# Startup loads of a linear-attention and FFN kernel: pieces over all 128 partitions, another order on the queues

## The reference

```
q = exp(x Wq.T + bq);  k = exp(x Wk.T + bk);  v = x Wv.T + bv
kv = cumsum over tokens of (k outer v);  k1 = cumsum over tokens of k
attention = (q . kv) / (q . k1), per head;  x = layernorm(x + attention Wo.T + bo)
h = ((x w) a1) a2;  x = layernorm(x + tanh(h + bias))
```

## Time and profile before

| | |
|---|---|
| median of three runs | 2304.31 us |
| the profiled execution | 2303.22 us |
| its span, first to last instruction | 2301.4 us |
| PE busy | 2241.9 us (97%) |
| DVE busy | 1617.2 us (70%) |
| POOL busy | 1294.2 us (56%) |
| ACT busy | 1012.3 us (44%) |
| mean granted clock of TensorE | 0.993 |
| DMA: share of 16 engines | 33.3% on SP's queue, 0.3% on ACT's |

### The profile page before, as it was taken

One profiled execution on the slowest core, in us unless ns is written; L12 is line 12 of the kernel. 1 busy time (PEld: TensorE's weight loads), 2 busy tenths in 40 slices (PEclk: granted clock), 3 DMA queues, 4 the chain that ended last, 5 costly groups with the idle time before them and its releaser, 6 DMA issues.

```text
span 2301.4 us, 77308 instructions
## 1 busy us (share of the span) xinstructions
PE 2241.9 (97%) x27752; PEld 1829.6 (80%) x27752; DVE 1617.2 (70%) x2456; ACT 1012.3 (44%) x1695; POOL 1294.2 (56%) x1797
## 2 busy tenths in 40 slices
PE   7999999999999999999999999999999999999985
PEld 6778888888888888888888888888888888887864
DVE  5576776776776776776776776776776776767674
ACT  4344444444444444444444444444444444444432
POOL 1356556556556556556556555555555555555554
PEclk9999999999999999999999999999999999999997
DMA  7133333333333333333333333333333333333221
GB/s 183 57 110 111 104 111 111 103 111 112 103 110 112 103 111 111 102 111 112 102 109 114 103 110 112 103 111 111 104 112 109 105 108 112 106 103 108 71 70 56
DMA packets 294574, 243.17 MB, mean 106 GB/s; under 512 B 33424, under 2 KB 225936, under 8 KB 294288
## 3 DMA queue, kind: packets, MB, share of 16 engines
q1 hardware_dynamic: 293136, 236.59, 33.3%
q10 hardware_dynamic: 1152, 2.10, 0.3%
HBM read 139.99 MB, written 98.57 MB: 104 GB/s over the span
## 4 chain that ended last, share of the span: by engine, by line
PE 95%; DVE 2%; issue 1%; SPq 1%; ACT 1%; DMA 1%; POOL 0%; POOLq 0%; DVEq 0%; ACTq 0%
PE SC L326 26%; PE SC L328 25%; PE SC L327 25%; PE SC L417 6%; PE ND L393 5%; PE ND L384 3%; PE ND L380 2%; PE ND L428 2%; DVE o L803 1%; DMA WK<-wT 0%; SPq L253 0%; ACT A L648 0%; DVE WK L816 0%; SPq L241 0%; PE ND L327 0%
## 5 line engine op out<-in xcount | busy, mean ns | idle before, releaser
L916 POOL TENSOR_SCALAR_AFFINE_SELECT A<-A 128x512 f32<-128x512 f32 x512 | 331.8, 682 | 321.1 <-ACT A L648 321.0
L803 DVE RECIPROCAL o<-ND 128x512 f32<-128x512 f32 x128 | 427.8, 3342 | 0.1
L857 DVE TENSOR_TENSOR xres<-SC,xres 128x512 f32<-128x512 f32 x128 | 88.5, 692 | 431.8 <-PE SC L328 431.6
L910 POOL TENSOR_TENSOR oL<-o,oH 128x512 fp32r<-128x512 f32 x128 | 166.4, 1300 | 327.0 <-ACT oH L627 327.0
L638 ACT ACTIVATE WK<-xres,shift,rstd 128x512 f32<-128x512 f32 x128 | 104.1, 814 | 531.7 <-POOL shift L951 531.7
L648 ACT ACTIVATE A<-SC 128x512 f32<-128x512 f32 x512 | 264.7, 603 | 43.3 <-PE SC L417 43.3
L326 PE MATMUL SC<-xTH,WqH 128*128 128x512 f32 x512 | 210.8, 412 | 9.5 <-ACT QT L598 3.7
L326 PE MATMUL SC<-WfH,x1H 128*128 128x512 f32 x512 | 201.0, 393 | 14.4 <-issue 7.9
L816 DVE TENSOR_TENSOR_SCAN WK<-ones,k,KT 128x128 f32<-128x128 f32 x512 | 207.5, 467 | 7.1 <-PE ND L380 6.8
L326 PE MATMUL SC<-WoH,oH 128*128 128x512 f32 x512 | 201.1, 393 | 11.3 <-issue 9.3
L598 ACT ACTIVATE QT<-SC,bcol 128x512 f32<-128x512 f32 x128 | 88.4, 690 | 270.4 <-PE SC L328 270.4
(11 more groups left out here) (103 smaller groups left out, 4983.3 us busy)
## 6 DMA issues: line engine op xcount, KB each, us to landing
xres<-x SPq DMA_DIRECT2D x128, 256.0 KB, 2.6
x_rows<-WK SPq DMA_DIRECT2D x128, 256.0 KB, 3.1
WK<-x_rows SPq DMA_DIRECT2D x512, 64.0 KB, 2.0
out<-WK SPq DMA_DIRECT2D x128, 256.0 KB, 2.0
xin<-x SPq DMA_DIRECT2D x504, 64.0 KB, 1.9
k_rows<-WK SPq DMA_DIRECT2D x120, 256.0 KB, 2.0
WK<-k_rows SPq DMA_DIRECT2D x480, 64.0 KB, 2.2
A<-a1T ACTq DMA_DIRECT2D x4, 256.0 KB, 5.4
```

Of the source, the lines that this page charges most:

```text
L803: nc.vector.reciprocal(o[:, :, :], den_ps).then_inc(recip_ready, 1)
L857: nc.vector.tensor_tensor(r, oproj_ps, r, ALU.add).then_inc(r_ready, 1)
L910: nc.gpsimd.tensor_tensor(oL[:, :, :], o[:, :, :], oH[:, :, :].bitcast(F32), ALU.subtract).then_inc(ol_ready, 1)
L916: last = nc.gpsimd.affine_select(out=A[:, k % 2, j, :, :], in_=A[:, k % 2, j, :, :], compare_op=ALU.is_ge, fill=0.0, base=0, pattern=[[0, ...
```

## The change

Every piece of x and of the four attention weights now fills all 128 partitions. A piece of x is one block of 32 tokens with its 4 feature groups: the source walks over 4 groups outermost, 32 tokens inside, 512 bytes each, and lands in 128 partitions by 512 bytes. A piece of a weight is one of four row sets: 4 groups outermost, 32 rows inside, 2048 bytes each, and lands in 128 partitions by 2048 bytes. Number and size of the pieces are the same. This holds for x in the loop as well.

SP now issues quarter 0 of a1T and a2, x 0, quarter 1, x 1, quarter 2, x 2, quarter 3, x 3, and then the biases, w, x 4, x 5, Wv, Wo and the rest as before. ACT issues Wq between its splits of quarters 0 and 1, and Wk behind that of quarter 1. ACT's `split_w` comes behind its first `keep_k`. DVE's `split_w` comes behind its `split_a12` and `turn_x` of tile 4, and its `split_wq_wk` 2 ahead of `turn_x` of tile 5.

```diff
@@ -45,7 +45,7 @@
     assert B == 2 * QUAD and NI >= 4
 
     x_t = x.rearrange("b (i p) d -> b i p d", p=P)
-    x_b = x.rearrange("b (i t p) (a f) -> b i a p t f", t=P // HD, p=HD, a=HG)
+    x_b = x.rearrange("b (i t p) (a f) -> b i t a p f", t=P // HD, p=HD, a=HG)
 
     k_rows = nc.dram_tensor("k_rows", [P, D], F32).ap()
     x1_rows = nc.dram_tensor("x1_rows", [P, D], F32).ap()
@@ -161,6 +161,12 @@
             early = c.static() and B * c.it + m in (2, 3)
             return V[:, m % 2, :] if early else xin[:, m % XIN, :]
 
+        def load_blocks(engine, tile, a, semaphore):
+
+            rows = a.rearrange("(a f p) n -> f a p n", a=HG, p=HD)
+            for f in range(NK):
+                engine.dma_start(tile[:, f, :], rows[f]).then_inc(semaphore, 16)
+
         def blocks_by_group(a):
             return a.rearrange("p (a m q) -> p m a q", a=HG, q=HD)
 
@@ -235,11 +241,6 @@
 
         @block.sync
         def _(sp):
-            def load_by_block(tile, a, semaphore):
-                rows = a.rearrange("(a f p) n -> a p f n", a=HG, p=HD)
-                for j in range(HG):
-                    sp.dma_start(tile[j * HD:(j + 1) * HD], rows[j]).then_inc(semaphore, 16)
-
             def load_biases():
                 sp.dma_start(bcol[:, 0, :], bq).then_inc(biases_loaded, 16)
                 sp.dma_start(bcol[:, 1, :], bk).then_inc(biases_loaded, 16)
@@ -249,9 +250,9 @@
                                      ).then_inc(biases_loaded, 16)
 
             def load_x(c, n):
-                for j in range(HG):
-                    sp.dma_start(x_buffer(c, n)[j * HD:(j + 1) * HD, :].rearrange("p (t f) -> p t f", t=HG),
-                                 x_b[n % B, c.it + n // B, j]).then_inc(xin_loaded[n % B], 16)
+                for t in range(HG):
+                    sp.dma_start(x_buffer(c, n)[:, t * P:(t + 1) * P],
+                                 x_b[n % B, c.it + n // B, t]).then_inc(xin_loaded[n % B], 16)
 
             def slot(c, k):
                 if c.exists(k - 2):
@@ -290,22 +291,28 @@
                     wait_before(sp, (out_ready, c.count(n + 1)))
                     sp.dma_start(out_t[n % B, c.it + n // B], y[:, n % 2, :]).then_inc(out_stored[n % B], 16)
 
+            def load_aux(f):
+                sp.dma_start(a1T_raw[:, f, :], a1T.rearrange("(k p) n -> k p n", p=P)[f]).then_inc(aux_loaded[f], 16)
+                sp.dma_start(a2_raw[:, f, :], a2.rearrange("(k p) n -> k p n", p=P)[f]).then_inc(aux_loaded[f], 16)
+
             first = Chunk(0)
+            load_aux(0)
             load_x(first, 0)
+            load_aux(1)
             load_x(first, 1)
-            load_by_block(wq_raw, wqT, wq_loaded)
+            load_aux(2)
             load_x(first, 2)
+            load_aux(3)
             load_x(first, 3)
-            load_by_block(wk_raw, wkT, wk_loaded)
             load_biases()
             sp.dma_start(w_raw, w.rearrange("(k p) n -> p k n", p=P)).then_inc(w_loaded, 16)
             sp.wait_ge(xl_ready, 1)
             load_x(first, 4)
             sp.wait_ge(xl_ready, 2)
             load_x(first, 5)
-            load_by_block(wv_raw, wvT, wv_loaded)
+            load_blocks(sp, wv_raw, wvT, wv_loaded)
             sp.wait_ge(auxl_ready, 2 * NK)
-            load_by_block(wo_raw, woT, wo_loaded)
+            load_blocks(sp, wo_raw, woT, wo_loaded)
             sp.dma_start(cbc[:], bo.partition_broadcast(P)).then_inc(small_loaded, 16)
             sp.dma_start(bfbc[:], bf.partition_broadcast(P)).then_inc(small_loaded, 16)
             for n in range(6, B + 1):
@@ -673,14 +680,10 @@
                 if att and not c.exists(k + 1):
                     split_o(k)
 
-            def aux_rows(a, f):
-                return a.rearrange("(k p) n -> k p n", p=P)[f]
-
-            for f in range(NK):
-                act.dma_start(a1T_raw[:, f, :], aux_rows(a1T, f)).then_inc(aux_loaded[f], 16)
-                act.dma_start(a2_raw[:, f, :], aux_rows(a2, f)).then_inc(aux_loaded[f], 16)
             split_aux(0)
+            load_blocks(act, wq_raw, wqT, wq_loaded)
             split_aux(1)
+            load_blocks(act, wk_raw, wkT, wk_loaded)
             split_x(*ahead(-8))
             split_aux(2)
             split_x(*ahead(-7))
@@ -689,13 +692,13 @@
             split_x(*ahead(-5))
             split_wq_wk(0)
             split_wq_wk(1)
-            split_w()
             split_a12()
             act.wait_ge(biases_loaded, 16 * (HG + 2))
             act.wait_ge(bq_ready, 1)
             keep_q(*ahead(-4))
             split_x(*ahead(-4))
             keep_k(*ahead(-4))
+            split_w()
             split_wq_wk(2)
             split_x(*ahead(-3))
             keep_q(*ahead(-3))
@@ -872,11 +875,11 @@
             split_wq_wk(0)
             split_wq_wk(1)
             prepare_biases()
+            split_a12()
+            turn_x(first, 4)
             split_w()
-            turn_x(first, 4)
-            split_a12()
+            split_wq_wk(2)
             turn_x(first, 5)
-            split_wq_wk(2)
             split_wq_wk(3)
             split_wv()
             turn_x(first, 6)
```

## The result

The changed kernel takes 2337.13 us (median of four runs, 2336.7 to 2339.67) against 2304.48 before: a ratio of 1.0145, with a 95% interval of 1.0127 to 1.0162. Its profiled execution took 2337.31 us, 34.09 more than that of before.

What follows compares the result with a forecast made beforehand. PE's own work was taken to bound the kernel (95% of the span), leaving only the start to change. The profiled 2303.22 plus 38.2 gave 2341.4, the median 1.1 above it: 2342 us, range 2322 to 2376.

Steps and rivals of the forecast that it cites:

- Four engines: Loads of x and attention weights: each new piece runs on the same four of 16 DMA engines; chance 0.79.
- The sum: Start of the kernel: waiting for x of tile 7 makes the scores of tile 0 come 38.2 us later.
- the landing of tile 7: Start: four engines need 83.7 us of packets from 2.7 us on, so x of tile 7 lands at 86.4.
- low end: Loads up to tile 7: overlapping packets give 74 in place of 83.7 us; with no clock loss, 2330.
- Case B: Loads of the start: four engines whose weight packets collide, 137 ns or 155 ns each, 2367 or 2376 us; chance 0.06.
- the low clock: PE from q of block 3 to the scores: 2.5 us more, as PE has stood before.
- The cover of the rest: Start: delays of 20 to 25 us to blocks 0 and 1 and `multiply_weight` end before PE's wait; nothing added.
- The loop: Slots of 17.3 us: x on four engines takes 3.3 us of data per slot, cost 0.
- the slack of the residual: Loop: the residual waits up to 3 us behind x but is read 15.8 us after its issue.
- Case A: Loads of the start: new pieces fill all 16 engines, 2296 us at full rate or 2300.7 at the old; chance 0.13.

Runs made afterwards that it cites:

- the runs with 2, 8 and 32: The changed kernel, x walked 32 outermost, weights 2 or 8 outermost: 2358.88 and 2305.86 us; with both x and weights 32 outermost: 2300.98 us.
- e10: The kernel before with only `split_w` moved on ACT and DVE as in the change: 2300.93 us, ratio 0.999.
- e11: e10 with Wq and Wk split over both queues, SP loading groups 0 and 1, ACT groups 2 and 3: 2298.87 us, ratio 0.9981.
- e2: The changed kernel with the pieces of before (32 partitions each), keeping the new order, queues and split order: 2306.93 us, ratio 1.0012.
- e4: The changed kernel with x walked 32 outermost and the weights as changed, so only the weights on four engines: 2321.15 us, ratio 1.0077.

## Why the prediction was right

**Four engines** was the step on which all hung, taken at 0.79 with no row that showed it; the share of 26.1%, the runs with 2, 8 and 32, and the count of packets show it. That they are the same four each time is shown by the stretches in which both queues have pieces under way: with changing ones their shares would have added up to more than 26.4%, and the packets wouldn't start in fours in turn.

**The sum.** It had 38.2 us up to the scores, and 33.7 were measured. The term that was too large is the landing of tile 7, 86.9 with its receipt, and DVE turned it at 82.7. Packets of 2048 bytes were taken at 89 ns, the price with all 16 engines busy, and cost 82: 512 x 7 ns = 3.6 us for the weights. x's were taken at 27.5, and from 76 to 80 us, when hardly anything else moved, cost 26.8 (686 packets at a share of 28.7%: 0.287 x 64 / 686). That is 0.7 us more, and with it nearly the 4.2 of difference. The fit is partly luck, for two things that the sum left out work against each other. Packets overlapped, 4.2 and 4.6 engines' worth of them on four, which the prediction used for its low end alone. And the engines weren't busy without a break: SP's first issues were to end by about 18 us, as they did before, and ended at 42.85; from 42 to 44 us only 46 GB/s moved, as w and x 4 were only being issued from 42.42 on. Case B's collisions didn't come; 82 ns is even less than the cheapest row had shown. The rest held: 5.8 us from the turn of tile 7 to q of block 3 (6.0 worked out), 11.3 from there to the scores (11.5), of which the low clock took 4.98 - 2.72 = 2.3 (2.5).

**The cover of the rest.** q and k of blocks 0 to 2 and `multiply_weight` end at about 75 us, and PE then stands until 88.55: the gains and losses of the other parts are lost in that wait, as worked out. The runs agree: with the new pieces, the old order takes 2337.8 us and the new one 2337.1.

**The loop** at 0 held, and the slack of the residual was the right row to ask.

**Case A was mis-sized.** It was to be 2296 with all 16 engines at full rate and 2300.7 at the old rate; the runs of just these two gave 2301.0 and 2306.9. The step that failed is that PE starts q of block 0 at 20.2: it started at 25.08 and 30.35, and `multiply_weight` at 36.55 and 41.82 in place of 32.6 and 37.2. The later `split_w` was worth what was said (e10); the loads weren't. I had read that the queues take turns packet by packet, and used it for the four engines only. With Wq and Wk on ACT's queue it also bears on which loads come late, though it doesn't explain e11 by itself. So even with 16 engines the change would have been within 0.2% of before, and the chance of faster, 0.09, was too high.

## What to carry to other kernels

Before a transfer is cut anew, write down the outermost count of its source: 4 groups outermost was four engines here, though the pieces filled 128 partitions. Then look at what is queued behind it, and who has to wait for the last of that. And a second queue isn't an overtaking lane for free: the one with the long packets takes most of the engines (77.7% against 33.1% in e2), so look at what is wanted first and shares them with something long that is wanted later. It can pay all the same, as e11 shows, which was the fastest kernel of all.

## What the runs showed of the hardware

Issuing a transfer can hold up its engine. Before, an issue on either queue took 0.4 to 0.5 us at the start, mostly. In the changed kernel, with the pieces backed up behind four engines, ACT's issues and its next split (start, duration):

```profile
12.49 10.89 ACTq L168 DMA_DIRECT2D KT<-wkT  x3
23.42 0.63 ACT L619 ACTIVATE xTH<-xin 128x512 fp32r<-128x512 f32 x1 [10.68 <-issue]
```

Three issues of Wk's pieces took 10.89 us, and `split_x` of tile 0 came only behind them, 10.68 us of idle time put down to issuing. SP's issue of quarter 2 of a1T took 3.14 us in the same way. The prediction had put ACT's eight issues at 3.6 us. They took 16.8 here, and 3.8 in the same order with the pieces of before (e2). In the changed kernel nothing was lost by it in the end, since PE had to wait for tile 7 anyway. With the weights alone on four engines (e4) PE did wait for it: ACT stood for 14.68 us put down to issuing, began its split of auxiliary quarter 2 at 24.37 without a wait for the data, and PE waited 12.44 us for that quarter. There too tile 7 came last. On an engine that also computes, such a wait could be the next bound.
